# Weight sums formed in DRAM during attention, and low halves of the gate and up weights made by accumulating DMAs

## The reference, cut to what matters

```python
x = _layernorm(x + _L0_attn_ref(x, Wq, Wk, Wv, Wo))
x = _layernorm(x + _L0_xattn_ref(x, tokens, ctx, ctx, ctx))   # expert of a token by its id
x = _layernorm(x + _L0_ffn_ref(x, w_gate, w_up, w_down))

def _L0_ffn_ref(x, w_gate, w_up, w_down):      # x 2048 rows of 512, I = 2048
    h = silu(x @ w_gate) * (x @ w_up)
    h_sparse = _sparsify_2to4(h)               # the two largest magnitudes of each four stay
    return h_sparse @ w_down
```

## Time and profile before

| | |
|---|---|
| Median of 3 runs | 1165.64 us (1163.32 to 1166.31) |
| Profiled execution, its own time | 1167.16 us |
| Its span, first to last instruction | 1165.1 us |
| Mean granted clock of PE | 0.954 |
| Busy: PE, PEld, DVE, ACT, POOL | 88%, 70%, 73%, 52%, 38% |
| DMA traffic | 146.14 MB |

### The profile page before, as it was taken

One profiled execution on the slowest core, in us unless ns is written; L12 is line 12 of the kernel. 1 busy time (PEld: TensorE's weight loads), 2 busy tenths in 40 slices (PEclk: granted clock), 3 DMA queues, 4 the chain that ended last, 5 costly groups with the idle time before them and its releaser, 6 DMA issues.

```text
span 1165.1 us, 18077 instructions
## 1 busy us (share of the span) xinstructions
PE 1022.4 (88%) x5830; PEld 820.7 (70%) x5831; DVE 848.2 (73%) x1857; ACT 606.0 (52%) x1141; POOL 441.4 (38%) x592
## 2 busy tenths in 40 slices
PE   7989999998998765998878598998988988998986
PEld 6667777776777644876767486786867767787764
DVE  5898799688788863654666948486587976949694
ACT  5787588478668841222435333443663434435423
POOL 2194457346446411353222223433111342615123
PEclk9999999999999977998989799998998998999998
DMA  8877267366627467488424125143230312414001
GB/s 259 246 201 191 82 191 218 91 199 173 173 82 188 167 223 210 118 204 229 133 68 153 49 61 82 36 77 77 64 100 28 91 46 64 136 56 133 27 20 73
DMA packets 73562, 146.14 MB, mean 125 GB/s; under 512 B 8065, under 2 KB 18305, under 8 KB 72321
## 3 DMA queue, kind: packets, MB, share of 16 engines
q1 hardware_dynamic: 67312, 122.45, 36.8%
q0 software_dynamic: 6160, 22.57, 7.1%
HBM read 114.05 MB, written 47.72 MB: 139 GB/s over the span
## 4 chain that ended last, share of the span: by engine, by line
PE 33%; DVE 17%; DMA 8%; ACT 3%; issue 2%; SPq 0%; POOL 0%; POOLq 0%; DVEq 0%; ACTq 0%
PE f_bank L1977 17%; PE f_bank L53 15%; DMA rows<-sorted_dram 4%; DVE beats L2345 3%; DMA w_raw<-gate 2%; DVE h L2369 2%; DVE h_lo L2378 2%; DVE w_lo L2266 1%; DVE rows_kept L2384 1%; DMA rows_kept<-ordered_dram 1%; ACT w_hi L2067 1%; DVE wins L2352 1%; DVE wins L2359 1%; ACT h_hi L2141 1%; DVE ln_stats L1104 1%
## 5 line engine op out<-in xcount | busy, mean ns | idle before, releaser
L1750 POOL TENSOR_TENSOR w_lo<-w_raw,w_hi 128x512 fp32r<-128x512 f32 x48 | 70.0, 1472 | 215.7 <-ACT w_hi L2067 215.6
L714 ACT ACTIVATE probs<-bank,nmax 128x384 f32<-128x384 f32 (+3 forms) x256 | 131.4, 547 | 21.0 <-DVE nmax L899 18.7
L883 DVE CUSTOM_DVE_ANT_0 bank<-bank,mask 128x384 f32<-128x384 f32 (+3 forms) x256 | 123.2, 503 | 13.3 <-PE bank L510 12.3
L521 PE MATMUL bank<-ident,probs 128*128 128x128 f32 x640 | 108.7, 284 | 24.3 <-DVE pt_lo L908 11.0
L908 DVE TENSOR_TENSOR pt_lo<-bank,pt_hi 128x512 f16<-128x512 f32 (+1 forms) x192 | 115.1, 599 | 16.6 <-ACT pt_hi L724 15.9
L1977 PE MATMUL f_bank<-x_hi_B,w_hi 128*128 128x512 f32 x192 | 80.8, 421 | 42.9 <-DVE h L2322 30.2
L724 ACT ACTIVATE pt_hi<-bank 128x512 f16<-128x512 f32 (+1 forms) x192 | 104.8, 546 | 23.5 <-PE bank L521 23.0
L53 PE MATMUL f_bank<-wd_hi,h_hi 128*128 128x512 f32 x256 | 101.9, 398 | 12.5 <-DVE h_lo L2378 7.1
L1977 PE MATMUL f_bank<-x_hi_T,w_hi 128*128 128x512 f32 x256 | 101.9, 398 | 11.3 <-ACT h L2114 11.2
L53 PE MATMUL bank<-x_hi,w_qk 128*128 128x512 f32 x256 | 101.2, 414 | 7.8 <-DVE x_lo L913 7.3
L1977 PE MATMUL f_bank<-x_lo_T,w_hi 128*128 128x512 f32 x256 | 101.4, 396 | 0.0
(11 more groups left out here) (275 smaller groups left out, 2738.1 us busy)
## 6 DMA issues: line engine op xcount, KB each, us to landing
w_raw<-sums_dram SPq DMA_DIRECT2D x64, 256.0 KB, 2.7
big_lo<-q_hi_dram SPq DMA_DIRECT2D x32, 256.0 KB, 3.8
big_lo<-q_lo_dram SPq DMA_DIRECT2D x32, 256.0 KB, 4.6
big_lo<-k_hi_dram SPq DMA_DIRECT2D x32, 256.0 KB, 3.7
big_lo<-k_lo_dram SPq DMA_DIRECT2D x32, 256.0 KB, 5.2
w_raw<-gate SPq DMA_DIRECT2D x32, 256.0 KB, 3.1
wd_raw<-down SPq DMA_DIRECT2D x32, 256.0 KB, 4.6
rows<-sorted_dram SPq DMA_DIRECT2D x19, 256.0 KB, 5.6
```

The costliest lines, as they stand in the source:

```text
L521: ins = pe.transpose(TP[u % TR][:, j * P:(j + 1) * P], probs[u % RP][:, j * P:(j + 1) * P], ident[:, :])
L714: ins = act.activation(probs[u % RP][:, at:at + cols(r)], S[u % SR][:, at:at + cols(r)], ACT.Exp, bias=nmax[:, r, c:c + 1])
L883: dve.tensor_tensor_reduce(out=S[u % SR][:, at:at + cols(r)], in0=S[u % SR][:, at:at + cols(r)], in1=mask[:, T - cols(r):T], scale=1.0, sc ...
L1750: pool.tensor_tensor(both(aw[1], X), both(raw, X), both(aw[0], X).bitcast(F32), ALU.subtract).then_inc(s_wlo[1], 1)
```

## The change

It has four parts. (a) The 8 MB of copies for the weight sums move into batch 1 of attention (16 DMAs of 512 KB on SP's queue, two behind each stack of q or k), and the 16 adds of 512 KB into batches 2 and 3 (on POOL's queue, one behind each head). `late` waits for them once, ahead of its first weight. (b) The low halves of all seven weight tiles are made otherwise: ACT copies `w_hi` into `w_lo` with scale -1 (`weight_minus`), and POOL issues a DMA that adds the weights from DRAM onto it. DVE's and POOL's subtractions are gone, 64 and 48 of them. (c) The tiles come in the order 1, 6, 5, 2, 7, 4, 3 instead of 1, 6, 5, 7, 2, 4, 3. (d) DVE's second chain, in an even round, is taken apart: `kept_lo` first, then `compare`, and the rest behind the round among the down product's additions. R8 keeps its chain. Some semaphores are merged or split.

```diff
+class WeightSums:
+    PIECES = 4
+        self.first = (up[0], up[0], gate[0], gate[1])
+        self.added = (up[1], gate[0], dram[0], dram[2])
...
+    def copy(self, sp, n):
+        i, q = divmod(n, self.PIECES)
+        sp.dma_start(self.rows(self.dram[i], q), self.rows(self.first[i], q)).then_inc(self.s_in, 16)
+
+    def add(self, pool, passed, n):
+        i, q = divmod(n, self.PIECES)
+        wait_apart(pool, passed, [(self.s_in, self.COPIED), (self.s_done, (0, 0, 8, 12)[i] * 16)] if i > 1
+                   else [(self.s_in, self.COPIED)])
+        pool.dma_start(self.rows(self.dram[i], q), self.rows(self.added[i], q), accum_op=ALU.add,
+                       max_dma_last_dim=8192).then_inc(self.s_done, 16)
...
@@ attention, POOL
+                        if b == 2 and c < 12:
+                            wsums.add(pool, s_passed_pool, c)
+                        if b == 3 and c < 4:
+                            wsums.add(pool, s_passed_pool, 12 + c)
@@ attention, SP
                 for g in range(G_AHEAD, 2 * NM):
                     stack_up(b, g)
+                    if b == 1:
+                        sums_at_first(g - G_AHEAD)
...
@@ late
-    FREED = ("1", "6", "5", "7", "2", "4", "3")
+    FREED = ("1", "6", "5", "2", "7", "4", "3")
-    LO_ON_POOL = ("6", "7", "4")
-    LO_ON_DVE = ("1", "5", "2", "3")
@@ late, POOL
             def weight_lo(L, X):
-                pool.wait_ge(s_whi, weight(L, X) + 1)
-                pool.tensor_tensor(both(aw[1], X), both(raw, X), both(aw[0], X).bitcast(F32),
-                                   ALU.subtract).then_inc(s_wlo[1], 1)
-
-            def sum_weights(at, of, units, waits):
+                n = weight(L, X)
+                waits = [(s_whi, 2 * n + 2)]
+                if n >= len(s_wlo):
+                    waits.append(ring(s_wlo, n - len(s_wlo)))
                 wait_apart(pool, s_passed, waits)
+                pool.dma_start(both(aw[1], X), weight_source(L, X), accum_op=ALU.add).then_inc(s_wlo[n % len(s_wlo)], 16)
@@ late, ACT
+            def weight_minus(L, X):
+                act.wait_ge(s_whi, 2 * weight(L, X) + 1)
+                act.activation(both(aw[1], X), both(aw[0], X).bitcast(F32), ACT.Copy, scale=-1.0).then_inc(s_whi, 1)
...
                 if more:
                     weight_hi(L + 1, "1")
+                    weight_minus(L + 1, "1")
@@ late, DVE
-            def weight_lo(L, X):
-                dve.wait_ge(s_whi, weight(L, X) + 1)
-                dve.tensor_tensor(both(aw[1], X), both(raw, X), both(aw[0], X).bitcast(F32),
-                                  ALU.subtract).then_inc(s_wlo[0], 1)
@@ late, DVE, early(L)
-                if L >= 2 and L % 2 == 0:
-                    chain = L - 1 if L != LB + 1 else L - 2
-                    compare(chain)
-                    count_first(chain)
-                    count_second(chain)
-                    choose(chain)
-                if L >= 2 and L != LB + 1:
+                if L == LB + 1:
+                    for way in (compare, count_first, count_second, choose):
+                        way(L - 2)
+                elif L >= 2:
                     kept_lo(L - 2)
+                if L >= 2 and L % 2 == 0 and L != LB + 1:
+                    compare(L - 1)
@@ late, DVE, behind(L)
-                ways = (compare, count_first, count_second, choose) if L % 2 == 1 or L == LB + 1 else ()
+                ways = (compare, count_first, count_second, choose) if L > 0 else (None,) * 4
+                if L % 2 == 0 and L != LB + 1:
+                    ways = (None,) + ways[1:]
```

More of the change, by code:

```diff
@@ L451, in batch, with sums_at_first @@
                         stack_up(b, g)
+                        if b == 1:
+                            sums_at_first(g - G_AHEAD)
+            def sums_at_first(n):
+                for i in (2 * n, 2 * n + 1):
+                    wsums.copy(sp, i)
             def qk_in(i):
@@ L1415, in cut_lo, with __init__, rows @@
         dve.tensor_tensor(self.lo[:, e], self.raw[e], self.hi[:, e].bitcast(F32), ALU.subtract).then_inc(self.s_lo, 1)
+class WeightSums:
+    PIECES = 4
+    def __init__(self, nc, ctx, dram, gate, up):
+        self.dram = dram
+        self.first = (up[0], up[0], gate[0], gate[1])
+        self.added = (up[1], gate[0], dram[0], dram[2])
+        self.s_in = ctx.enter_context(nc.semaphore("s_sums_in"))
+        self.s_done = ctx.enter_context(nc.semaphore("s_sums"))
+        self.COPIED = self.PIECES * len(self.first) * 16
+        self.DONE = self.PIECES * len(self.first) * 16
+    def rows(self, t, q):
+        units = t.shape[0] // self.PIECES
+        return t[q * units:(q + 1) * units].rearrange("u p n -> (u p) n")
+    def copy(self, sp, n):
[7 more added lines that the diff above has]
+                       max_dma_last_dim=8192).then_inc(self.s_done, 16)
 def late(nc, big_at, rows_kept, context, ident, tile_expert, slot_idx, place_idx, sorted_rows, s_sc, ordered_rows,
-         order_dram, sums_dram, gate, up, down, out_rows, N, E, D, I):
+         order_dram, wsums, gate, up, down, out_rows, N, E, D, I):
     KT = D // P
@@ L1567, in late @@
         s_pr, s_cp, s_ad = sem("s_product"), sem("s_copied"), sem("s_added")
[L1568 to L1569 removed]
+        s_h1 = sem("s_h_r1")
+        s_mag, s_ch = sem("s_mag"), sem("s_ch")
         s_acc = sem("s_facc")
@@ L1784, in _ @@
                 place(n)
-                for sum_of in sums_at.get(n, ()):
-                    sum_weights(*sum_of)
-                if n in first_weight and first_weight[n] in LO_ON_POOL:
+                if n in first_weight:
                     weight_lo(0, first_weight[n])
@@ L1941, in product @@
                 if name[1] == "a":
-                    pe.wait_ge(*wlo_ready(L, which))
+                    pe.wait_ge(*ring(s_wlo, weight(L, which)))
                 if L % (2 * NCH) == 0 and name[1] == "a":
@@ L2093, in step @@
                 act.activation(gt[0][i][:, :, :].rearrange("p k t -> p (k t)"), EG[i][:, :],
-                               ACT.Copy).then_inc(s_gh, 1)
+                               ACT.Copy).then_inc(s_hi, 1)
                 if isinstance(n, int) and n in first_weight:
                     weight_hi(0, first_weight[n])
+                    weight_minus(0, first_weight[n])
                 if isinstance(n, int) and n == 15:
@@ L2156, in round_ @@
                 s, odd = divmod(L, 2)
-                more = L + 1 < MADE
+                more = L + 1 < ROUNDS
                 copy(L, "1a")
@@ L2187, in round_ @@
                     weight_hi(L + 1, X)
+                    weight_minus(L + 1, X)
                 if L >= 2 and not odd:
@@ L2200, in round_ @@
                 silu(L, 1, 1)
-                for X in ("7", "2", "4") if more else ():
+                for X in ("2", "7", "4") if more else ():
                     weight_hi(L + 1, X)
+                    weight_minus(L + 1, X)
                 if L == LB:
@@ L2211, in round_ @@
                     weight_hi(L + 1, "3")
+                    weight_minus(L + 1, "3")
             for n in range(2):
@@ L2375, in kept_lo @@
                 for half in range(2):
-                    dve.wait_ge(s_hh, 2 * d + half + 1)
+                    dve.wait_ge(s_hi, NS + 2 * d + half + 1)
                     k = hslot[2 * s + half, r]
```

112 lines of the change are left out of this document (40 added, 72 removed).

## The result

The changed kernel is slower: median 1180.08 us (1179.38 to 1182.66, four runs) against 1164.48 us (1162.14 to 1166.31, four runs) on the same chip, ratio 1.0139, 95% interval [1.0119, 1.016]. The forecast was 1154, faster than before, with a range of 1138 to 1170. The profiled execution has a span of 1178.8 us, 13.7 more than before.

The account below looks back on a forecast made before the run. PE, busiest at 88%, bounds the kernel with its idle and low-clock stretches. Terms -25 + 2 + 10.8 + 0 + 7 - 6 - 1 + 1 = -11.2 take 1167.2 to 1156.0 us, median 1154.5, stated 1154; range 1138 to 1170.

Parts of the forecast that it names:

- (a) Expert tiles: Expert tiles: without copies and adds, row loads land in time and the stalls with their low clock go, 25 us less.
- (a) Attention: Attention: the moved copies and adds cost 2 us, bounds 0 and 6, as stacks are loaded two groups ahead.
- Attention pays: Rival, attention: POOL is full in batch 2, its head sums hold ACT and PE, 13 us; total 1165; chance 0.10.
- (b) The landing: Ahead of "2a" in R1, R2, R15: accumulating DMA lands in 5 us, "2a" 3.4 us later; 10.8 us without R2.
- The rival "late": Rival, rounds: accumulating DMAs land late, costing from 10 us on; 1170 at 10.5 us, 1190 at 12; chance 0.13.
- (d) R4 and R6: R4 and R6: `beats` must follow `h_lo` behind ACT's slow load, 3.5 us more each, 7 in all, bounds 2 and 12.
- R2: R2's stall of 12.4 us: part of DVE's second chain leaves, so it ends 6 us earlier, bounds 3 and 12.
- R10 to R13: Even rounds R10, R12, R14: `beats` slowed beside POOL's `wd_lo`, so nothing won, 0 us, bounds -12 and +3.

Follow-up runs that it names:

- e1: Kernel before the change with only the sums' copies and adds moved into attention; ratio 0.9893 to the kernel before.
- e5: Changed kernel with each of the sixteen adds covering 64 of its 256 rows (128 instead of 512 KB); ratio 1.0078 to the kernel before.
- e6: Changed kernel with copies behind SP's batches 0 and 1, eight adds between batches 2 and 3, eight in expert tiles 2 to 9; ratio 1.0013 to before.
- e7: Changed kernel with down's four 256 KB loads ahead of R1's weight loads and the last block's 1 MB load a round later; ratio 1.0277 to before.
- e4: Changed kernel with DVE's chains in the order of before; ratio 1.0095 to the kernel before.
- e13: e10 with the low half of tile 2 alone made by a subtraction on DVE; ratio 0.9774 to the kernel before.
- e11: e9 with DVE's chains in the order of the change; ratio 0.9717 to the kernel before, median 1137.2 us.
- e3: Changed kernel with the low halves made by DVE's and POOL's subtractions again; ratio 0.9985 to the kernel before.
- e8: Changed kernel with the sixteen scatters of 4-byte entries moved from POOL's rounds 2 to 5 into expert tiles 2 to 9; ratio 0.9991 to before.
- e10: Changed kernel with the sums at e6's places and the sixteen scatters of 4-byte entries in attention; ratio 0.9809 to the kernel before.
- e9: Kernel before with the sums at e6's places and the sixteen scatters of 4-byte entries in attention; ratio 0.9778 to the kernel before.
- e2: Changed kernel with the sums put back between the expert tiles; ratio 1.0274 to the kernel before.

## Why the prediction was wrong

**(a) Expert tiles: right.** -27.8 against -25. The stalls for rows and `rows_kept` went with their low clock, and e1 shows it for the sums alone.

**(a) Attention: wrong, the step "The q and k stacks are loaded two groups ahead, which covers a DMA that is some us late. I take 2 us".** It cost 14.7, with the reads of the stacks waiting for their writes (9.9 and 10.5 us instead of 5.2 and 6.2). I had read DMA shares of 0.69 and 0.71 and added the traffic to nothing. The adds bring the share to 1.0, and a k pair makes two trips one behind the other, to DRAM and back, so that being two groups ahead isn't enough. The rival "Attention pays" had the place and almost the size, with the wrong mechanism: POOL's issue time is innocent (e5), the bytes at this place do it (e5, e6). This step alone is 12.7 of the 25 us by which the profiled executions missed the sum.

**(b) The landing: mechanism right, a term mis-sized at one place.** I had 5 us for it everywhere, and "2a" 3.4 us later: 2.5 for ACT's copy and 0.9 for the landing behind it. "2a" came 8.3, 2.7 and 2.8 us later in R1, R2 and R15. The copy's part was 3.6, 2.5 and 2.0 us, near the 2.5; the landing's part was 4.6, 0.2 and 0.8 us. It took 4.5 and 4.1 us in R2 and R15, well met, and 9.1 in R1, because I hadn't looked at what SP issues in those microseconds. e7 shows the 2 MB as the cause. The low clock behind each of the stalls (0.73 and 0.50 in the windows at 610 and 637) adds to it. Of the 6.4 us at R14 to R15, 1.9 stand already in R14; with DVE's old order these two rounds are 3.8 us shorter (e4), and why isn't shown.

The Trainium skill, page "DMA: Bandwidth & Descriptors", section "Anatomy of one DMA — SWDGE (gpsimd) path", gave an estimate of 2.6 us; the measured 4.1 to 9.1 decide, and it has no term for neighbours. The rival "late" priced landings from 10 us on, by rounds that have a down product; the three without one pay earlier. With tile 2's landing taken away, the late copy stays: 5.04 against 1.38 us in R1 (e13, e11).

**Not in the sum: R3 and R5, +9 us, a term that I put at nothing.** I had counted POOL's added issues, but not what stands behind them on its queue. Before, R3's four scatters were issued by 678.3, the load of `w_raw` that ACT needs came at 682.30 and landed in 6.5 us, in time. After, the scatters are issued from 670.7 to 676.2, around that load (675.14), and it takes 11.0 us. With subtractions again both waits vanish (e3), and with the scatters elsewhere too (e8). e8 takes 24.8 us off the changed kernel's rounds by moving the scatters alone, more than R3 and R5, since R4's and R6's waits were of this kind too.

**(d) R4 and R6: right in sum** (+8.2 for 7), partly by luck: the new wait at "3a" was 2.60 and 1.69 us instead of 3.5, and R6's wait for ACT at "4a" grew from 4.53 to 7.11. **R2:** its stall gave -10.8 and the later "2a" ahead of it cost 5.4, -5.4 together for the -6 that I had for both. **R10 to R13: near** (-1.9 for 0), and the price is where I had put it, `beats` at 5.66 instead of 3.49 us beside POOL. The Trainium skill, page "SBUF — State Buffer", section "Who interferes with whom", says that such a pair shuts each other out; the trace agrees in direction, with 2.2 us lost by `beats`.

**The net.** Attention and the wait behind it +15.0, tiles -27.8, rounds +26.4: 13.6, for 13.7. The sums' part brought 13 us (e1 has 1.1%), the rest cost 26. Of these 26, e8 takes back 24.8 in the rounds by moving the scatters alone, but pays 10.0 in the tiles. With the scatters out of both, the rest costs 4.7 us (e10 over e9), and this is a sum of two terms: -8.3 for the order on DVE (e11 over e9) and +13.0 for the accumulating DMAs with their tile order (e10 over e11). Of the 13, about 7 are tile 2's low half in R1 and R2 (e13). The other 6 are a net sum: R1, R14 and R15 still lose 12.6 us, with ACT's late copy in R1 and R15, and the other rounds gain 8.6 (e13 over e11); that leaves 4, and 2 more stand in R10 to R12. No run parts these.

**Open.** The rounds of kernels that differ only outside them took 602.6, 610.1 and 612.1 us (changed, e6, e2), mostly in the waits for `w_raw` in R4 and R6, and those of e5 615.7. A meeting of scatters and loads that depends on some microseconds would do this, but no run isolates it. So a few us between the rounds of two kernels, as the 4.0 of e13 over e11, are no firm number. Attention's loss too varies between executions, 10.2 to 17.5 us with the same adds (e1, e8).
